# GpSimd adds beta to x after 48 of its 180 trailing scatters, not after all of them: a graph network's node stage on Trainium2

## Chip, cores and metric

The kernel runs on 1 core of one Trainium2 chip, in one launch. The metric is device time in microseconds (us), median over runs. Engines by their names in the profile: PE is TensorE (PEld its weight load), DVE VectorE, ACT ScalarE, POOL GpSimd, SP SyncE, which here only issues DMAs.

## What is computed

A heterogeneous graph attention layer (4 node types, 6 relations, 8 heads), a residual with layer norm, then three graph convolutions with batch norm over the same edges, and a last residual with layer norm. There are N = 6250 nodes of 128 features and E = 106250 edges, sorted by destination. Cut to what matters here:

```python
x = layernorm(x + L0(x, src, dst, node_type, edge_type, ...))
x = layernorm(x + L1(x, edge_index, edge_weight, ...))

# the end of L0, for each node
h = typed_linear(h, Wa, ntype)
gate = sigmoid(skip)[ntype]
y = x + h * gate + x * (1 - gate)
L0 = (y - mu) / sqrt(var + 1e-5) * ln_gamma + ln_beta

# L1, three times
agg = segment_sum((x @ W)[src] * norm, dst) + b
x = relu(batch_norm(agg))        # the last one without relu
```

The outer residual adds x to the normalised y * gamma + beta. The kernel therefore forms x + beta once, for all nodes, and adds it to y * gamma.

## The kernel before

Nodes lie in 49 row tiles of 128, edges in 832 tiles of 128 in the order of their destinations, batched by 16 tiles into NB = 52 batches. The program has these stages, in order of time: tables of keys and values per node (to 650 us or so); the attention over the 52 batches (to 1990); the **node stage**, which this change touches; three graph convolution layers (2286 to 4470); and the last norm.

In the layers the first T1 = 320 edge tiles are done densely. Their weights were written beforehand into a table in HBM, `a_tab`, a piece of the adjacency matrix with 13 chunks of up to 512 columns by 49 row tiles. The table is zeroed early, and then 320 **scatters** on GpSimd (line 481, one indirect DMA for each edge tile, 128 single words, each with `cells_saved`) put the sums in their cells. The first 140 of them are spread over the attention, one before each group of four gathers from batch SB = 17 on (line 494). The other 180 are issued in one loop behind the last gather (lines 505 and 506). Behind that loop GpSimd waits for `y_set` (509) and adds beta to x in the tile `xr`, 128 x 6272 elements in one instruction (510), which raises `xb_ready`. Its next work is the gathers of layer 0 (523), behind `tab_complete`.

VectorE in the node stage: it scales the attention's sums (1391), writes y = x * keep from `xr` and raises `y_set` (1394), adds the four types' parts of h (1406) and takes the moments of each row tile (1411), makes mean, variance and shift of the first normalisation (1419 to 1431), then waits for `xb_ready` (1437). For each chunk of four row tiles it then multiplies by gamma (1442), adds `xr` (1443) and takes the moments (1445); each chunk also waits for ScalarE's first normalise, `y_normed` (683). ScalarE's second normalise writes x1 over `xr`. TensorE turns x1 (954, 957), computes its product with W (981), VectorE scales these rows by the degree into `xr` (1463) and clears the sums (1465). With that, layer 0's dense products (997) can start, as far as their A blocks are loaded. TensorE adds the blocks' own part with the identity (1002) and interleaves the products of gathered edges (969).

SyncE issues in a written order. It waits for `cells_saved` of all 320 scatters and for `types_done` (418, 419). Then, for each layer, it issues NBUF = 4 A blocks of 7 row tiles (416), 12 + 1 stores of h rows to `h_tab` (427, 431) each behind its `hrow_ready`, waits for all of these stores, raises `tab_complete` (433), and issues the remaining 87 A blocks, each behind `a_used`, since there are four buffers.

SyncE's code in front of the layers:

```python
sp.wait_ge(cells_saved, 16 * T1)
sp.wait_ge(types_done, NT)
for l in range(3):
    for b in range(NBUF):
        a_block(l, b)
```

Of the kernel before, what the change touches and what calls it, by code (L numbers as in the profile page):

```python
# [18 lines left out]
NG = TPB // GRP  # L19

T1 = 320
# [3 lines left out]
PACE = 5  # L25
QSTEP = 9
SB = 17
ZB = 2


# [28 lines left out]
def gnn(nc, x, src, dst, etype, ew, ntype, Wk, Wq, Wv, Wa, rel_pri, rel_att, rel_msg, skip, gamma, beta,  # L59
# [13 lines left out]
    NB = ET // TPB  # L73
# [30 lines left out]
    with ExitStack() as ctx:  # L104
# [3 lines left out]
        def sem(name):  # L108
# [16 lines left out]
        sizes = (("big", 2 * TPB * 2 * D), ("relb", TPB * P), ("negs", 4 * P), ("qwin", TPB * D), ("ohT", 2 * GRP * P),  # L125
                 ("bd", 2 * R * D), ("wkqv", 3 * T * D), ("xmT", 4 * T * D), ("qkv", 6 * D), ("square", 5 * P), ("wa", T * D))
        arena = sb("arena", [P, sum(n for _, n in sizes)])
        at, part = 0, {}
        for name, n in sizes:
# [94 lines left out]
        zero_set, a_zeroed, a_rest_zeroed, cells_saved = (  # L224
            sem(n) for n in ("zero_set", "a_zeroed", "a_rest_zeroed", "cells_saved"))
        at = sum(n for _, n in sizes[0:5])
        zero = arena[:, at:at + KB * 256]
        ZT = 61
# [218 lines left out]
        def _(pool):  # L447
# [32 lines left out]
            def scatter(t):  # L480
                G.indirect_dma_start(a_tab, bass.IndirectOffsetOnAxis(cell[:, t:t + 1], 0), tot[:, t:t + 1], None)\  # L481
                 .then_inc(cells_saved, 16)

            def gather(b):
                pool.wait_ge(idx_ready, b + 1)
                pool.sem_inc(gathers_begun, 1)
                if b == SB:
                    pool.wait_ge(a_zeroed, 16 * ZT)
                    pool.wait_ge(a_rest_zeroed, 16 * (NBLK - ZT))
                    pool.wait_ge(tot_ready, 1)  # L490
                    pool.wait_ge(cell_ready, 1)
                for g in range(NG):
                    if b >= SB:
                        scatter(NG * (b - SB) + g)
                    if b >= 3:
                        pool.wait_ge(vw_ready, NG * (b - 3) + g + 1)
                        pool.sem_inc(gathers_begun, 1)
                    for s in range(GRP):
                        t = g * GRP + s
                        G.indirect_dma_start(kv[b % 3][:, t, :], None, kv_tab,  # L500
                                             bass.IndirectOffsetOnAxis(idxr[:, b % 3, t:t + 1], 0))\
                         .then_inc(kv_land[b % 3][g], 16)
            for b in range(NB):
                gather(b)
            for t in range(NG * (NB - SB), T1):
                scatter(t)


            pool.wait_ge(y_set, 1)
            G.tensor_tensor(xr[:, :, :], xr[:, :, :], lnw[:, 1:2, :].to_broadcast([P, NT, D]), ALU.add).then_inc(xb_ready, 1)  # L510

            for l in range(3):
                pool.wait_ge(tab_complete, l + 1)
# [3 lines left out]
                for q in range(GQ):  # L517
# [3 lines left out]
                    for s in range(GRP):  # L521
                        t = T1 + q * GRP + s
# [5 lines left out]
        def _(act):  # L528
# [105 lines left out]
            def attend(b, i, par, peeled):  # L634
                al.at((TPB + NG) * (b - 1) + NG + 2)
                for z in range(ZT + ZB * (b - 1), min(NBLK, ZT + ZB * b)):
                    act.dma_start(a_flat[z, :, :].rearrange("p (a f) -> p a f", a=2),
# [947 lines left out]
```

## Time and profile before

| | |
|---|---|
| median of 3 runs | 4505.61 us (4501.09 to 4509.4) |
| profiled execution, its own time | 4512.08 us |
| its span, first to last instruction | 4510.3 us |
| PE busy | 3479.3 us, 77% of the span |
| POOL busy | 2626.3 us, 58% |
| DVE busy | 2379.0 us, 53% |
| ACT busy | 900.6 us, 20% |
| mean granted TensorE clock | 0.863 |

All times below count from the start of the span, in us. A timeline row has start, duration, engine, line, operation, output<-inputs and count; in brackets stands how long the engine had been idle before it, and what ended that. A row with a count above 1 merges instructions that follow one another. In a row of a DMA the duration is that of the issue on its engine, not of the transfer. Line numbers are those of the kernel before; in the changed kernel the lines from the new constant on are higher by 1, and those behind the new loop by 3.

### The profile page before, as it was taken

The numbers are of one execution on the slowest core, as the hardware profiler recorded it, in microseconds if no ns is written. First come the engines' busy times: TensorE is split into PE (matmuls) and PEld (weight loads), VectorE is DVE, ScalarE is ACT, GpSimd is POOL, SyncE is SP. The second block draws the span as 40 slices with busy tenths as digits, with TensorE's granted clock in tenths as the row PEclk, the third lists the DMA queues.
The fourth block names the chain that finished last, engine by engine and source line by source line (L and its number), as shares of the span: only waits on it lengthen the run. The fifth ranks groups of instructions, "written<-read, shape, count | busy, mean of one in ns | idle before, by whom it ended". The sixth has DMA issues, their size and how long they took to land.

```text
span 4510.3 us, 56344 instructions
## 1 busy us (share of the span) xinstructions
PE 3479.3 (77%) x16302; PEld 2387.8 (53%) x16302; DVE 2379.0 (53%) x7762; ACT 900.6 (20%) x2048; POOL 2626.3 (58%) x2767
## 2 busy tenths in 40 slices
PE   2688856666666666663099999969999978999993
PEld 2577755666665565651055555545555545555552
DVE  2333336667777777774245544455544444554446
ACT  0111124555555555531100000000000000000001
POOL 0000036556777777777447677746777764767772
PEclk8799977777877777777599999979999989999996
DMA  7777757776555555420168788858788867878881
GB/s 261 271 312 305 298 187 272 269 272 198 159 143 157 146 151 152 144 71 1 65 240 299 288 297 302 300 173 308 293 294 296 302 232 256 295 289 297 296 295 49
DMA packets 367669, 1041.17 MB, mean 231 GB/s; under 512 B 77923, under 2 KB 250264, under 8 KB 324610
## 3 DMA queue, kind: packets, MB, share of 16 engines
q1 hardware_dynamic: 251090, 660.52, 40.7%
q0 software_dynamic: 108112, 321.99, 21.2%
q10 hardware_dynamic: 8160, 55.05, 3.2%
q8 instruction: 133, 2.18, 0.2%
q14 instruction: 174, 1.43, 0.1%
HBM read 808.64 MB, written 228.66 MB: 230 GB/s over the span
## 4 chain that ended last, share of the span: by engine, by line
PE 45%; DVE 3%; POOL 1%; issue 1%; DMA 0%; ACT 0%; POOLq 0%; DVEq 0%
PE bank L997 36%; PE bank L969 7%; POOL stage L523 1%; PE bank L1002 1%; DVE nodes L1535 1%; DVE sums L1534 1%; DVE xr L1463 0%; DVE sums L1465 0%; DVE xr L1556 0%; PE bank L981 0%; DMA stage<-h_tab,earr 0%; DVE nodes L1553 0%; DVE sums L1550 0%; PE bank L1015 0%; DVE sums L1503 0%
## 5 line engine op out<-in xcount | busy, mean ns | idle before, releaser
L523 POOL DMA_INDIRECT stage<-h_tab,earr x1536 | 1452.7, 946 | 778.3 <-issue 361.9
L997 PE MATMUL bank<-arena,xr 128*128 128x512 f32 (+1 forms) x3822 | 1693.9, 590 | 9.1 <-DVE xr L1463 9.1
L997 PEld LDWEIGHTS bank<-arena,xr 128*128 128x128 f32 x3822 | 697.8, 191 | 722.2 <-issue 712.6
L1503 DVE TENSOR_TENSOR sums<-sums,bank 128x128 f32 x1536 | 435.6, 284 | 781.1 <-PE bank L969 776.3
L500 POOL DMA_INDIRECT arena<-kv_tab,idxr x560 | 539.9, 964 | 301.7 <-issue 167.8
L1474 DVE TENSOR_SCALAR oh<-iota_j,earr 128x128 f32<-128x128 f32 x1536 | 586.7, 385 | 90.6 <-DVE sums L1494 43.1
L969 PEld LDWEIGHTS bank<-oh,stage 128*128 128x128 f32 x3072 | 408.9, 196 | 236.1 <-issue 190.3
L969 PE MATMUL bank<-oh,stage 128*128 128x128 f32 x3072 | 421.5, 282 | 51.8 <-DMA stage<-h_tab,earr 41.8
L665 ACT ACTIVATE rs<-mv,epsc 128x49 f32<-128x49 f32 (+1 forms) x6 | 1.9, 317 | 2241.2 <-DVE mv L1537 2015.4
L838 PE MATMUL bank<-arena 128*128 128x128 f32 x1664 | 255.9, 310 | 190.1 <-issue 99.1
L481 POOL DMA_INDIRECT a_tab<-tot,cell x320 | 320.9, 1003 | 100.2 <-issue 100.2
L1294 DVE TENSOR_TENSOR sums<-sums,bank 128x256 f32 x832 | 347.8, 418 | 55.0 <-DVE sums L1294 10.4
L838 PEld LDWEIGHTS bank<-arena 128*128 128x128 f32 x1664 | 232.6, 220 | 197.0 <-issue 189.1
L477 POOL DMA_DIRECT2D a_tab<-sums x61 | 32.5, 536 | 518.9 <-ACT stage L561 462.3
L500 POOL DMA_INDIRECT xr<-kv_tab,idxr x272 | 264.5, 972 | 113.2 <-issue 79.6
L852 PE MATMUL bank<-oh,stage 128*128 128x128 f32 x1664 | 292.6, 332 | 34.0 <-issue 21.5
L852 PEld LDWEIGHTS bank<-oh,stage 128*128 128x128 f32 x1664 | 262.7, 240 | 52.5 <-issue 51.0
L1494 DVE TENSOR_TENSOR sums<-sums,stage 128x1 f32 x960 | 154.8, 161 | 219.8 <-DVE sums L1494 62.9
L604 ACT ACTIVATE oh<-iota_j,earr 128x128 f32<-128x128 f32 x832 | 262.5, 386 | 5.4 <-PE bank L855 5.4
L855 PE MATMUL bank<-oh,arena 128*128 128x128 f32 x1664 | 259.5, 308 | 0.0
L855 PEld LDWEIGHTS bank<-oh,arena 128*128 128x128 f32 x1664 | 245.4, 226 | 0.0
L595 ACT ACTIVATE arena<-arena,iota_p 128x512 f32<-128x512 bf16 x208 | 148.1, 712 | 203.6 <-PE bank L838 197.1
(216 smaller groups left out, 3228.4 us busy)
## 6 DMA issues: line engine op xcount, KB each, us to landing
arena<-a_tab SPq DMA_DIRECT2D x273, 1792.0 KB
a_tab<-sums POOLq DMA_DIRECT2D x61, 1792.0 KB, 9.3
a_tab<-arena ACTq DMA_DIRECT2D x30, 1792.0 KB
arena<-q_tab SPq DMA_DIRECT2D x832, 64.0 KB
kv_tab<-stage SPq DMA_DIRECT2D x48, 768.0 KB, 4.7
arena<-rel_d SPq DMA_DIRECT2D x52, 512.0 KB, 5.0
stage<-h_tab,earr POOLq DMA_INDIRECT x1536
h_tab<-xr SPq DMA_DIRECT2D x36, 256.0 KB
```

What stands on the lines that cost most here:

```text
L481: G.indirect_dma_start(a_tab, bass.IndirectOffsetOnAxis(cell[:, t:t + 1], 0), tot[:, t:t + 1], None)\
L500: G.indirect_dma_start(kv[b % 3][:, t, :], None, kv_tab, bass.IndirectOffsetOnAxis(idxr[:, b % 3, t:t + 1], 0))\
L523: G.indirect_dma_start(gring[:, (q % NG) * GRP + s, :], None, h_tab[l], bass.IndirectOffsetOnAxis(src_i[:, t:t + 1], 0)).then_inc(row_land ...
L604: al.inc(S.activation(oh[:, g, s, :], iota_j[:, :], ACT.Abs, scale=-1.0, bias=rel_c[:, bass.ds(c * TPB + (g * GRP + s), 1)]))
L838: last = M.matmul(bank[g % 2][:, s * D:(s + 1) * D], ohT[:, g % 2, s * P:(s + 1) * P], qwin[:, g * GRP + s, :], start=True, stop=True)
L852: M.matmul(o_[s][:, P:2 * P], exw[:, g * GRP + s, :], oh[:, g, s, :], start=True, stop=True)
L855: last = M.matmul(o_[s][:, 0:P], vw[:, g * GRP + s, :], oh[:, g, s, :], start=True, stop=True)
L969: last = M.matmul(bank[q % NG][:, s * P:(s + 1) * P], gring[:, (q % NG) * GRP + s, :], oh[:, q % NG, s, :], start=True, stop=True)
L997: mm = M.matmul(o_[:, 0:cw], xr[:, n, :], abuf[B % NBUF][:, n % KB, 0:cw], start=n == 0, stop=n == NT - 1)
L1294: V.tensor_tensor(w_, w_, d_.rearrange("p (k j) -> p k j", k=2), ALU.add).then_inc(acc_added, 1)
L1474: V.tensor_scalar(oh[:, q % NG, s, :], iota_j[:, :], rel_c[:, t:t + 1], ew_c[:, t:t + 1], ALU.is_equal, ALU.mult).then_inc(wt_ready, 1)
L1503: V.tensor_tensor(w_, w_, bank[q % NG][:, s * P:(s + 1) * P], ALU.add).then_inc(win_added, 1)
```

## The change

GpSimd's loop over the 180 trailing scatters is cut in two. It issues SY = 48 of them, waits for `y_set`, adds beta to x, and then issues the other 132. Nothing else is changed.

```diff
 SB = 17
+SY = 48
 ZB = 2
...
             for b in range(NB):
                 gather(b)
-            for t in range(NG * (NB - SB), T1):
+            for t in range(NG * (NB - SB), NG * (NB - SB) + SY):
                 scatter(t)
 
 
             pool.wait_ge(y_set, 1)
             G.tensor_tensor(xr[:, :, :], xr[:, :, :], lnw[:, 1:2, :].to_broadcast([P, NT, D]), ALU.add).then_inc(xb_ready, 1)
+            for t in range(NG * (NB - SB) + SY, T1):
+                scatter(t)
 
             for l in range(3):
                 pool.wait_ge(tab_complete, l + 1)
```

GpSimd's instructions from the last scatter and gathers of the attention on, before (`a_tab` takes the scatters, `lnw` holds gamma and beta, `arena` here the gathered keys and values):

```order
L481 DMA a_tab<-tot,cell 41746432x1
L500 DMA arena<-kv_tab,idxr 128x256 x4
L481 DMA a_tab<-tot,cell 41746432x1 x180
L510 TENSOR_TENSOR xr<-xr,lnw 128x6272
L523 DMA stage<-h_tab,earr 128x128 x1536
```

And in the changed kernel:

```order
L482 DMA a_tab<-tot,cell 41746432x1
L501 DMA arena<-kv_tab,idxr 128x256 x4
L482 DMA a_tab<-tot,cell 41746432x1 x48
L511 TENSOR_TENSOR xr<-xr,lnw 128x6272
L482 DMA a_tab<-tot,cell 41746432x1 x132
L526 DMA stage<-h_tab,earr 128x128 x1536
```

The add has moved ahead of 132 scatters; the gathers of the layers stay behind both.

SyncE's instructions around the start of the layers, in the changed kernel (`in_x` is x, loaded again into `xr` once the attention has left it):

```order
L408 DMA xr<-in_x 128x32x128
L417 DMA arena<-a_tab 128x3584 x4
L428 DMA h_tab<-xr 128x4x128 x12
L432 DMA h_tab<-xr 106x128
L417 DMA arena<-a_tab 128x3584 x91
```

Nothing has moved there: four A blocks, which wait for the last scatter, stand ahead of the stores of h, and the fifth block (of the 91, 87 belong to layer 0) stands behind them, as before.

## Rows read from the trace of the kernel before

**Rows 1.** The page, section 4: the chain that ended last, by engine and by line

```profile
PE 45%; DVE 3%; POOL 1%; issue 1%; DMA 0%; ACT 0%; POOLq 0%; DVEq 0%
PE bank L997 36%; PE bank L969 7%; POOL stage L523 1%; PE bank L1002 1%; DVE nodes L1535 1%; DVE sums L1534 1%; DVE xr L1463 0%; DVE sums L1465 0%; DVE xr L1556 0%; PE bank L981 0%; DMA stage<-h_tab,earr 0%; DVE nodes L1553 0%; DVE sums L1550 0%; PE bank L1015 0%; DVE sums L1503 0%
```

**Rows 2.** Timeline of VectorE in the node stage

```profile
2011.89 6.69 DVE L1394 TENSOR_TENSOR arena<-xr,keep 128x6272 f32<-128x6272 f32 x1
2018.61 2.16 DVE L1406 SCALAR_TENSOR_TENSOR arena<-bank,gmask,arena 128x128 f32<-128x128 f32 x8
...
2082.75 0.21 DVE L1431 SCALAR_TENSOR_TENSOR shf<-mv,rs 128x49 f32<-128x49 f32 x1
2208.72 0.69 DVE L1442 TENSOR_TENSOR arena<-arena,lnw 128x512 f32<-128x512 f32 x1 [125.76 <-POOL xr L510]
2209.44 0.69 DVE L1443 TENSOR_TENSOR arena<-arena,xr 128x512 f32<-128x512 f32 x1
```

**Rows 3.** Timeline of GpSimd in the node stage

```profile
1956.84 1.00 POOL L481 DMA_INDIRECT a_tab<-tot,cell  x1 [0.30 <-issue]
1958.14 1.21 POOL L481 DMA_INDIRECT a_tab<-tot,cell  x1 [0.30 <-issue]
...
2012.63 6.79 POOL L481 DMA_INDIRECT a_tab<-tot,cell  x1 [0.31 <-issue]
2019.72 0.97 POOL L481 DMA_INDIRECT a_tab<-tot,cell  x1 [0.30 <-issue]
...
2194.30 0.96 POOL L481 DMA_INDIRECT a_tab<-tot,cell  x1 [0.30 <-issue]
2195.28 13.40 POOL L510 TENSOR_TENSOR xr<-xr,lnw 128x6272 f32<-128x6272 f32 x1
```

**Rows 4.** Timeline of ScalarE: its first normalise

```profile
2083.00 18.94 ACT L683 ACTIVATE arena<-arena,shf,rs 128x128 f32<-128x128 f32 x49 [0.78 <-DVE shf L1431]
```

**Rows 5.** SyncE's waits, 1950 to 2500: total, times, longest

```profile
SPq L416 <- DMA a_tab<-tot,cell: 119.5, 1, 119.5
...
SPq L433 <- DMA h_tab<-xr: 2.8, 1, 2.8
```

**Rows 6.** Timeline of SyncE's DMA issues, 1950 to 2500

```profile
2196.46 1.85 SPq L416 DMA_DIRECT2D arena<-a_tab  x4
2273.86 12.30 SPq L427 DMA_DIRECT2D h_tab<-xr  x12
2286.48 0.30 SPq L431 DMA_DIRECT2D h_tab<-xr  x1
```

**Rows 7.** Timeline of TensorE at the start of layer 0

```profile
2286.51 1.86 PE L997 MATMUL bank<-arena,xr 128*128 128x448 f32 x2 [3.39 <-DVE xr L1463]
...
2288.59 31.41 PE L997 MATMUL bank<-arena,xr 128*128 128x448 f32 x78
```

**Rows 8.** Timeline of VectorE in the attention's last batches

```profile
1957.80 1.29 DVE L1271 TENSOR_TENSOR arena<-xr,stage 128x512 f32<-128x512 f32 x2 [0.17 <-ACT stage L623]
```

**Rows 9.** Source line 500, the gathers: ns min/median/max, first and last start

```profile
L500 POOL DMA_INDIRECT xr<-kv_tab,idxr x272: 942/946/1474, 660.6 to 1930.2; - x136
```

**Rows 10.** Busy time by stage (windows), columns in the first row

```profile
core 0: us, PE busy (x) PEld busy (x) DVE busy (x) ACT busy (x) POOL busy (x), PEclk, DMA share, GB/s
...
2209.00:2258.00 49.00, 0.21 (x1) 0.21 (x2) 28.34 (x84) 19.54 (x51) 0.00 (x0) 0.50 0.12 53
2197.00:2215.00 18.00, 0.00 (x0) 0.00 (x0) 6.08 (x16) 0.00 (x0) 11.68 (x1) 0.50 0.98 407
2275.00:2286.00 11.00, 8.12 (x73) 7.92 (x71) 10.45 (x21) 0.00 (x0) 0.00 (x0) 0.98 0.86 242
2286.00:2290.00 4.00, 3.49 (x6) 1.94 (x7) 2.99 (x12) 0.00 (x0) 0.12 (x1) 0.50 0.43 120
2320.00:3003.00 683.00, 645.59 (x2314) 355.21 (x2313) 342.51 (x1380) 1.61 (x4) 469.13 (x496) 0.97 0.76 281
```

**Rows 11.** Source line 477, stores of 1792 KB: us to landing

```profile
DMA to landing us min/median/max: 6.9/9.3/41.1
```

## The prediction

> **What bounds the kernel now.** I read the page's chain first: the matmuls of the three layers and of their edge groups (L997, L969) carry 43% of the span, GpSimd 1%, and no line of the node stage has as much as 1% [rows 1]. So an edit in the node stage pays only if it makes layer 0 start earlier; after that the layers should run as before.
>
> In the timelines of the node stage the reader is to see two engines side by side. VectorE writes y = x times its gate at 2011.89 to 2018.58, which raises y_set, then works through y_rows, and has mean, variance and shift of the first normalisation by 2082.96 [rows 2]. It then stands until 2208.72, 125.8 us, for GpSimd. GpSimd meanwhile issues 180 scatters, one per 1.27 us, from 1956.84 to 2195.26, and only then makes the add, 13.40 us [rows 3]. ScalarE's first normalise ran 2083.00 to 2101.94 and is no cause of the wait [rows 4]. But there is a second reader of the scatters: SyncE waited 119.5 us until all of them had landed, then issued the first four A blocks at 2196.46 [rows 5, 6]. Today these blocks lie ready long before TensorE takes the first at 2286.51 [rows 7]. That cover is what the change uses up.
>
> **The change, part by part.**
>
> The add is neither cheaper nor dearer: 1 instruction, 13.40 us. When is it reached? The scatter at 2012.63 is the 44th of the 180, the one at 2019.72 the 45th [rows 3] ((2012.63 - 1956.84) / 1.27 = 43.9 behind the first); the 48th then starts at 2019.72 + 3 x 1.27 = 2023.5 and ends at 2024.5. y_set was up at 2018.6, so the new place of the wait costs 0, with 5.9 us to spare. The add runs 2024.5 to 2037.9 and VectorE needs it at 2083 or later: the 125.8 us wait is gone. VectorE's next limit is ScalarE: the first four rows of 49 are normalised 4 x 0.39 = 1.6 us after 2083.0, so VectorE restarts at 2084.6 instead of 2208.7, and all that hangs on it (second moments, second normalise, transposes, layer 0's rows of h) comes 124.1 us earlier. The last row of h, written just before 2286.5, is ready at 2162.
>
> Behind the add on GpSimd stand 132 scatters. All of them come 13.4 us later, so the last ends at 2208.7 and not at 2195.3. The scatters are DMA issues; the A blocks (SyncE L416) wait for all 320, and the 13 h_tab stores stand behind these blocks in SyncE's own order. So here is what is late next: SyncE cannot send h_tab, though its rows are ready from 2162, before the last scatter has landed.
>
> To the 13.4 us comes a term that the trace of before shows only in small. VectorE's L1442 and L1443, two SBUF operands each, now run at 2084.6 to about 2113 beside scatters and no longer beside an empty GpSimd. The scatter that began 0.74 us into the 6.69 us L1394 (also two SBUF operands) took 6.79 us instead of 0.97 and ended 0.84 us after it [rows 2, 3]. The one at 1958.14, beside the short L1271, took 1.21 us [rows 3, 8]; the worst gather took 1.474 us against a median of 0.946, 0.53 us more [rows 9]. So a scatter is held until the VectorE instruction ends. VectorE's loop is busy for 28.3 us [rows 10], 23 scatters long; L1442 and L1443 take 1.38 us in some 2.2 us of each chunk, or 0.63 of the time. I take half of that worst case: 23 x 0.63 x 0.27 = **4 us**. Bounds: 0, and 26 instructions x 0.53 = 14 us. For the 6.7 us of L1394 nothing changes, since it meets the 44th scatter in both kernels.
>
> The Trainium skill, "SBUF — State Buffer", section "Who interferes with whom", says that a VectorE instruction with two SBUF inputs contends with a GpSimd instruction that reads SBUF, but that tensor_tensor leaves the generation of DMA descriptors alone, which it marks as inferred. By its second half this term would be 0 and the time 4447.6; the 6.79 us row speaks for the first half, and I go by the row.
>
> So the A blocks go out at 2196.46 + 13.42 + 4 = **2213.9** (call it T).
>
> From T on, with durations from rows:
> - The four blocks are 7.34 MB. In before the DMA engines were 0.98 busy at 407 GB/s for them from 2197 to 2215.3 [rows 10]: the reads end at T + 18.9. The first block should land at about T + 6.9, the shortest landing of any transfer of that size [rows 11].
> - TensorE starts then. Its first 28 row tiles (four blocks of seven) took from 2286.51 to 2288.59 + 54 x 0.40 = 2310.3 in before [rows 7], 23.8 us. So it runs out of blocks at T + 30.7.
> - The 13 h_tab stores, 3.2 MB, queue behind the reads. They moved at 242 GB/s with 0.86 of the engines' time [rows 10], so 3.2 / 0.281 = 11.4 us when nothing paces them, plus 2.8 us for the last to land [rows 5]: T + 33.1, and 0.4 us for the signal and the issue.
> - Only then do the blocks from the fifth on go out (SyncE's order: blocks, h_tab, blocks), and GpSimd's row gathers too. The fifth lands 6.9 us later, T + 40.4. TensorE stands for about 10 us, which in before it did not.
> - After a pause of 3.4 us at 2286 the granted clock was 0.50 for about 4 us [rows 7, 10], the lower of the two levels, 1.2 GHz. I count one such start more, 4 us at half speed: 2 us.
>
> TensorE's 29th row tile is reached at 2213.9 + 40.4 + 2.0 = 2256.3 against 2310.3: **54.0 us earlier**. From there both kernels do the same work. GpSimd's gathers start some 7 us before the fifth block and TensorE needs the first group only at row 40, some 18 us after that start, so it has no lack. The granted clock in the layer was 0.97 [rows 10]; I leave it.
>
> The sum against the profiled execution, 4512.08: 4458.1. That execution lies 6.5 above the median, 4505.61, and by the median the forecast is **4451.6**, 4452 rounded.
>
> So of 125.8 us of waiting less than half is paid out: 124 us earlier on VectorE, of which 70 go back to scatters 17.4 us later, the landing of the blocks, and h_tab behind them.
>
> **The rivals.**
>
> 1. No starving at the fifth block (0.12). If stores and reads share the DMA engines without slowing each other, h_tab is complete before TensorE has used four blocks, and only T + 6.9 + 23.8 counts: 2244.6, 65.7 us earlier, 4440. For it: SyncE issues the 13 stores within some 6 us of T. Against it: the engines were 0.98 busy with the reads alone.
>
> 2. The add is slowed by VectorE (0.11). In before it ran while VectorE did nothing; now it runs beside y_rows. If it took twice its time, every scatter behind it and so T comes 13.4 us later: 40.6 us earlier, 4465. Against: scatters beside y_rows kept their pace of 1.27 us, and L1406 has one operand in PSUM.
>
> 3. Slower than before (0.03). One mechanism: L1442 and L1443 hold the scatters as L1394 did, by 6.79 - 0.97 = 5.8 us in each of 13 chunks, together 76 us in place of my 4. Then T is 2285.9 and the gain of 54 turns into 18 us lost, 4524. It decides from 58 us in all, 4.5 us a chunk. Against: the hold ends with the instruction, and these last 0.69 us, not 6.69.
>
> 4. The whole wait is won (0.02): 4505.6 - 124.1 = 4381.5. It would need SyncE's blocks not to depend on the last scatter; the 119.5 us wait says they do.
>
> 5. The add does not leave the path, within 0.2% (0.02): y_set might be read late or the 48th scatter come before it. Then GpSimd stands for some us, VectorE still goes at 2084.6; only if the scatters end after 2268 is nothing won.
>
> **How the numbers follow.** My own case has 0.70. Its bounds: the hold 0 to 14 us, -4 and +10; h_tab 5 us faster or slower; the slow clock 0 to 4. Together about 4440 to 4467. With rivals 1 and 2 and the noise of the median I give **4434 to 4470**, which leaves out rivals 3 to 5 and the tails. The three runs shown spread by 0.2%; that is about what a measurement tells from no change. Faster by more than that: 0.70 + 0.12 + 0.11 + 0.02 = 0.95; same 0.03 (rival 5 and part of 3); slower 0.02.
>
> **What would show it.** Right: the add at about 2024.5, still 13.4 us long; L1442 starting near 2085 with no GpSimd wait; the last scatter ending near 2213 and SyncE's first blocks right behind; TensorE's first wait in layer 0 for those blocks, a second of about 10 us before the fifth, and from there the same pace. Scatters between 2085 and 2113 longer than 0.97 us. Wrong: scatters slowed by more than 14 us, an add over 14 us, a layer 0 that from row 28 on takes over 5 us more or less than before, or first matmuls that start at 2162 already.

## The result, and the profile after

| | before | changed |
|---|---|---|
| median (runs) | 4507.50 us (4) | 4449.89 us (4), 4448.37 to 4452.93 |
| ratio, 95% interval | | 0.9874 [0.9857, 0.9892] |
| span of the profiled execution | 4510.3 us | 4448.6 us |

The change saves 57.6 us by the medians and 61.7 us between the two profiled executions, of which the one before took 4.6 us more than its median and the changed one 0.4; forecast were 54.0. The page's chain now runs back through the scatters and gathers (L482 has 7% of it), which it did not before [rows 1]:

```profile
PE 52%; POOL 21%; issue 10%; DMA 9%; DVE 5%; SPq 2%; ACT 1%; POOLq 0%; DVEq 0%; ACTq 0%
```

In all rows of the changed kernel the lines are higher by 1 to 3 (L482 is the scatter, L511 the add, L1397 the write of y, L1445 and L1446 the two instructions of VectorE's chunk loop, L1000 the dense product). GpSimd's timeline, against [rows 3]:

```profile
1955.26 0.98 POOL L482 DMA_INDIRECT a_tab<-tot,cell  x1 [0.30 <-issue]
...
2011.46 7.09 POOL L482 DMA_INDIRECT a_tab<-tot,cell  x1 [0.30 <-issue]
...
2022.36 13.48 POOL L511 TENSOR_TENSOR xr<-xr,lnw 128x6272 f32<-128x6272 f32 x1
...
2088.10 0.96 POOL L482 DMA_INDIRECT a_tab<-tot,cell  x1 [0.30 <-issue]
2089.37 1.38 POOL L482 DMA_INDIRECT a_tab<-tot,cell  x1 [0.30 <-issue]
2091.05 1.20 POOL L482 DMA_INDIRECT a_tab<-tot,cell  x1 [0.30 <-issue]
...
2207.76 0.96 POOL L482 DMA_INDIRECT a_tab<-tot,cell  x1 [0.30 <-issue]
```

The add stands in the middle of the scatters, no slower than alone, and with no wait ahead of it. After two of 1.02 and 1.19 us at 2085.29 and 2086.61 the scatters repeat the pattern of the three rows at 2088.10 until 2110: 0.96, 1.38, 1.20 us. VectorE's timeline, against [rows 2]:

```profile
2011.03 6.68 DVE L1397 TENSOR_TENSOR arena<-xr,keep 128x6272 f32<-128x6272 f32 x1
...
2082.00 0.21 DVE L1434 SCALAR_TENSOR_TENSOR shf<-mv,rs 128x49 f32<-128x49 f32 x1
2084.00 0.75 DVE L1445 TENSOR_TENSOR arena<-arena,lnw 128x512 f32<-128x512 f32 x1 [1.78 <-ACT arena L686]
```

The wait of 125.76 us for GpSimd has become one of 1.78 us for ScalarE. SyncE's issues, against [rows 6], and then TensorE, against [rows 7]:

```profile
2209.92 1.85 SPq L417 DMA_DIRECT2D arena<-a_tab  x4
2211.82 24.66 SPq L428 DMA_DIRECT2D h_tab<-xr  x12
2236.53 0.80 SPq L432 DMA_DIRECT2D h_tab<-xr  x1
2240.78 57.12 SPq L417 DMA_DIRECT2D arena<-a_tab  x11
```

```profile
2216.78 1.83 PE L1000 MATMUL bank<-arena,xr 128*128 128x448 f32 x2 [57.70 <-DMA arena<-a_tab]
...
2218.84 21.17 PE L1000 MATMUL bank<-arena,xr 128*128 128x448 f32 x54
2247.92 10.79 PE L1000 MATMUL bank<-arena,xr 128*128 128x448 f32 x24 [7.92 <-DMA arena<-a_tab]
2258.55 1.05 PE L972 MATMUL bank<-oh,stage 128*128 128x128 f32 x8
```

TensorE waits for the first A block, 57.7 us, runs through four blocks (2 + 54 instructions are 28 row tiles), stands 7.9 us for the fifth, and goes on. After both pauses TensorE began at the lower of the two clock levels (windows; PEclk, the granted clock, is the third column from the end):

```profile
2216.00:2220.00 4.00, 3.22 (x6) 1.93 (x7) 0.00 (x0) 0.00 (x0) 0.00 (x0) 0.50 1.02 437
2247.00:2252.00 5.00, 4.08 (x7) 2.08 (x8) 0.00 (x0) 0.00 (x0) 3.77 (x4) 0.60 1.03 413
```

The stores of h went out between the first four blocks and the fifth, at a higher rate than in before (the last column is GB/s):

```profile
2230.00:2236.00 6.00, 6.00 (x17) 3.04 (x16) 0.00 (x0) 0.00 (x0) 0.00 (x0) 1.00 1.14 341
```

The first group of gathered edges, which in before began at 2319.84, begins at 2258.55, 61.3 us earlier; the first products of the other two layers come 61.7 and 61.1 us earlier, and the span is 61.7 us shorter.

### The profile page after: what moved, and what is told of

Its sections match the earlier page's. It is cut to its first block, busy times and chain, and to the rows that moved or that the text cites. A ratio compares the mean times of both kernels' runs of the same rounds, so it can differ in the third digit from the quotient of the medians.

```text
span 4448.6 us, 56344 instructions
## 1 busy us (share of the span) xinstructions
PE 3491.4 (78%) x16302; PEld 2399.4 (54%) x16302; DVE 2378.4 (53%) x7762; ACT 900.5 (20%) x2048; POOL 2624.3 (59%) x2767
## 4 chain that ended last, share of the span: by engine, by line
PE 52%; POOL 21%; issue 10%; DMA 9%; DVE 5%; SPq 2%; ACT 1%; POOLq 0%; DVEq 0%; ACTq 0%
PE bank L1000 36%; POOL arena L501 8%; PE bank L972 8%; POOL a_tab L482 7%; DMA q_tab<-arena 6%; POOL xr L501 4%; DMA negb_d<-arena 2%; PE bank L855 2%; PE bank L858 1%; PE bank L841 1%; POOL stage L526 1%; PE bank L784 1%; PE bank L1005 1%; DVE nodes L1538 1%; PE bank L795 1%
## 5 line engine op out<-in xcount | busy, mean ns | idle before, releaser
L1000 PE MATMUL bank<-arena,xr 128*128 128x512 f32 (+1 forms) x3822 | 1696.0, 590 | 71.4 <-DMA arena<-a_tab 65.6
L1000 PEld LDWEIGHTS bank<-arena,xr 128*128 128x128 f32 x3822 | 698.7, 191 | 785.8 <-issue 771.0
L482 POOL DMA_INDIRECT a_tab<-tot,cell x320 | 320.9, 1003 | 100.1 <-issue 100.1
```

Of the source, the lines that this page charges most:

```text
L1000: mm = M.matmul(o_[:, 0:cw], xr[:, n, :], abuf[B % NBUF][:, n % KB, 0:cw], start=n == 0, stop=n == NT - 1)
```

## The experiments

Two theories stood against each other. **A**: the end follows the last of two things, the last scatter (with the A blocks behind it) or VectorE's rows of h; in the changed kernel it is the last scatter, so nothing that VectorE does matters. **B**: the end follows VectorE's restart. Beside them, **C**: the stop at the fifth block, which A puts down to the stores' place in SyncE's order, comes from DMA engines that are busy with reads.

The first four ran together, with 15 runs of the kernel before at 4510.47 us. VectorE's timelines show where the loop restarts, SyncE's where the first A blocks go out (T), TensorE's the rest. Since the first of the 180 scatters starts up to 8 us apart from one execution to the next (1948.96 in e4, 1956.84 in before), T is also given from the first of the 180 scatters (in e1, which has none there, from the last gather's start + 1.25 us). "Stop" is TensorE's wait for the fifth block, and the last column ends at its first group of gathered edges.

| | SY | median us | restart | T | T from first | first product | stop | T to first group |
|---|---|---|---|---|---|---|---|---|
| changed | 48 | 4449.89 | 2084.0 | 2209.92 | 254.7 | T + 6.9 | 7.9 | 48.6 |
| e1 | 0 | 4508.55 | 2084.3 | 2266.96 | 311.3 | T + 6.9 | 8.4 | 50.5 |
| e2 | 100 | 4449.54 | 2096.8 | 2205.50 | 254.8 | T + 7.0 | 8.8 | 50.8 |
| e3 | 48 | 4437.69 | 2079.1 | 2205.03 | 254.6 | T + 7.3 | none | 39.1 |
| e4 | no add | 4443.75 | 2077.4 | 2193.13 | 244.2 | T + 7.0 | 7.0 | 49.8 |

**e1: the add ahead of all 180.**

```diff
-SY = 48
+SY = 0
```

> The add ahead of all 180 scatters. GpSimd is through with the gathers at about 1955 and must wait for y_set until 2017.7, then add until 2031.2, then issue 180 scatters at 1.262 us with 3.6 us of hold and one gap of 2.7: the last ends near 2265, SyncE's first A blocks go out near 2266. Theory A (the end follows the last scatter, whatever VectorE does): everything from the first A block on 56 to 57 us later than in the changed kernel, about 4506 us, no better than before the change, although VectorE still restarts at 2084. Theory B (the end follows VectorE's restart, which the change moved from 2208.7 to 2084): the same restart, so about 4450.

4508.55 us, ratio to before 0.9996 [0.9987, 1.0005]. VectorE restarts as early as in the changed kernel, and all of the gain is gone. This alone settles A against B. GpSimd's and SyncE's rows:

```profile
2018.40 13.47 POOL L511 TENSOR_TENSOR xr<-xr,lnw 128x6272 f32<-128x6272 f32 x1 [63.02 <-DVE arena L1397]
```

```profile
2266.96 1.80 SPq L417 DMA_DIRECT2D arena<-a_tab  x4
```

GpSimd stands 63 us with 180 scatters behind it. Counted from the end of the gathers T is 56.6 us later; 56 to 57 were worked out.

**e2: the add behind 100.**

```diff
-SY = 48
+SY = 100
```

> The add behind 100 of the 180 scatters. It starts near 2088 and ends near 2101.5, so VectorE restarts 18 us later than in the changed kernel (2083.8). The number of instructions ahead of the last scatter is the same, so it ends where it did, 2208.7 within 2 us. Theory A (last scatter): time unchanged, 4450 within 4. Theory B (VectorE's restart): 18 us later, 4468.

4449.54 us: no change. The wait for GpSimd is back in VectorE's timeline, 19.12 us where the changed kernel waited 1.78, so VectorE restarts 17 us later than it could, at no cost:

```profile
2096.82 0.69 DVE L1445 TENSOR_TENSOR arena<-arena,lnw 128x512 f32<-128x512 f32 x1 [19.12 <-POOL xr L511]
```

T from the first scatter is 254.8 us, against 254.7. Between 48 and 100 scatters ahead of the add nothing is gained or lost.

**e3: the stores ahead of the A blocks, in layer 0.**

```diff
-            sp.wait_ge(cells_saved, 16 * T1)
             sp.wait_ge(types_done, NT)
             for l in range(3):
-                for b in range(NBUF):
-                    a_block(l, b)
+                if l:
+                    for b in range(NBUF):
+                        a_block(l, b)
...
                 sp.sem_inc(tab_complete, 1)
-                for b in range(NBUF, NBLK):
+                if l == 0:
+                    sp.wait_ge(cells_saved, 16 * T1)
+                for b in range(NBUF if l else 0, NBLK):
                     a_block(l, b)
```

> In layer 0 alone, SyncE issues the 13 stores of h and raises tab_complete before it waits for the last scatter, and only then issues A blocks. Theory A (the 7.9 us stop before the fifth A block comes from the stores that queue behind four blocks and hold the fifth back): the stores land near 2165, the stop and the slow clock after it go, TensorE's 29th row tile comes 8 to 9 us earlier, about 4441 us. Theory C (the fifth block is late because the DMA engines are busy with reads, stores or not): a stop of 5 us or more stays, 4447 to 4450.

4437.69 us, 12 us less than e2 and than the changed kernel, the fastest version of the study and faster than both kernels (ratio to before 0.9844 [0.9831, 0.9857]). The stop is gone, so A holds and C falls:

```profile
2144.96 12.25 SPq L428 DMA_DIRECT2D h_tab<-xr  x12
2157.54 0.29 SPq L432 DMA_DIRECT2D h_tab<-xr  x1
2205.03 122.59 SPq L417 DMA_DIRECT2D arena<-a_tab  x21
```

```profile
2212.30 1.83 PE L1002 MATMUL bank<-arena,xr 128*128 128x448 f32 x2 [58.12 <-DMA arena<-a_tab]
...
2214.35 29.98 PE L1002 MATMUL bank<-arena,xr 128*128 128x448 f32 x78
2244.17 1.05 PE L974 MATMUL bank<-oh,stage 128*128 128x128 f32 x8
```

The 78 instructions behind the first tile run in one piece of 29.98 us, where the changed kernel took 21.17 + 10.79 = 31.96 beside its stop: 7.9 of stop and 2.0 of slow clock. From T to the first group it is 9.5 us shorter than in the changed kernel's trace. Against e1 and e2 it is 11.4 and 11.7 us shorter, close to the 12 of the medians, because there the stop and the low clock behind it lasted longer: in the changed kernel the low clock was over after 3 us, in e1 it held through the whole of this window:

```profile
2305.00:2311.00 6.00, 5.58 (x8) 2.71 (x9) 0.00 (x0) 0.00 (x0) 4.48 (x6) 0.50 1.01 405
```

The same 24 products behind the stop took 10.8 us in the changed kernel and 12.2, 12.0 and 11.7 in e1, e2 and e4.

**e4: beta added on VectorE, chunk by chunk, and no add on GpSimd.**

```diff
-            pool.wait_ge(y_set, 1)
-            G.tensor_tensor(xr[:, :, :], xr[:, :, :], lnw[:, 1:2, :].to_broadcast([P, NT, D]), ALU.add).then_inc(xb_ready, 1)
...
-            dve.wait_ge(xb_ready, 1)
...
                 dl.link(V.tensor_tensor(y_, y_, xr[:, n0:n1, :], ALU.add))
+                dl.link(V.tensor_tensor(y_, y_, lnw[:, 1:2, :].to_broadcast([P, n1 - n0, D]), ALU.add))
```

> GpSimd makes no add; VectorE adds beta in its chunk loop instead, 13 further additions of 0.69 us (the sum is rounded in another order). VectorE ends its part some 9 us later, which its slack of 48 us before the last scatter covers. GpSimd's 132 scatters come 13.5 us earlier, less what the 13 new instructions with two SBUF operands hold them, 2 us. Theory A: first A blocks near 2198, 11 to 12 us less than the changed kernel, about 4438. Theory B (VectorE's chain): 9 us later, 4459.

4443.75 us, but its four runs lie between 4433.6 and 4448.4, so the median says only that it is not slower. The trace is sharper: T comes 10.5 us sooner after the first scatter, expected were 11 to 12. Of the 3 us that are missing of the 13.5, about 2 went to the hold, which three instructions with two SBUF operands in each chunk make nearly continuous. As much again went to a slower pace of all scatters in this execution, 1.274 us from one to the next where the changed kernel had 1.262, and 0.7 came back, because the scatter beside the long write of y was held less (6.36 us in place of 7.09). Before, too, ran at 1.273; why an execution has one pace or the other is not shown. GpSimd beside VectorE's loop in e4:

```profile
2083.66 1.19 POOL L482 DMA_INDIRECT a_tab<-tot,cell  x1 [0.30 <-issue]
2085.16 1.15 POOL L482 DMA_INDIRECT a_tab<-tot,cell  x1 [0.31 <-issue]
```

These two alternate until 2113.16; every scatter there takes 1.14 us or more, one 1.41.

**e5 to e12: other chips.** The next two sets of four ran on two other chips, where the kernel before takes 5442.9 and 5447.0 us. They were meant to extend the first set; e9 to e12 are the kernels of e6, e5, e7 and e8 again. The times that their expectations name were worked out for a kernel before at about 4508 us. None of these four kernels ran on the first chip, so what they were to test there stays untested, above all theory A's turning point in e7: that with SY = 140 VectorE's rows become the later of the two sides and the time 4450 to 4458.

> SyncE's order of the third experiment put on the kernel before, where the add is still behind all 180 scatters. There the rows of h are ready only at 2286.5, 90 us after the last scatter. The four A blocks that used to lie ready are now issued at about 2290, behind the wait for the stores, and land 6.9 us later: TensorE's first product of layer 0 comes 10 us later. Theory A (an order of the queue is worth what it is only together with which of the two, scatters or rows, is late): slower than before by 8 to 11 us, 4516 to 4520. If the stores-first order were better by itself: 4500 or less.

> The add on VectorE (fourth experiment) and the stores first (third) together. By theory A the two are terms of one path, the last scatter and what stands between it and the 29th row tile, and add up: 11 to 13 us from the first and 8 to 12 from the second, 4427 within 5 us, the fastest so far. VectorE's rows of h are ready near 2165, still 28 us before the last scatter.

> The add behind 140 of the 180 scatters: it ends near 2151, VectorE's rows of h are ready 78 us later, near 2229, now later than the first A block (2216.8 in the changed kernel). Theory A with the point where it ends (the later of last scatter and VectorE's rows decides): the first product 12 us later, but the stores are no longer packed behind the blocks, so the stop before the fifth block shrinks; 4450 to 4458. Theory B: 4450 + 67 = 4517, since VectorE restarts 67 us later.

> In VectorE's chunk loop the two instructions with two SBUF operands, y times gamma and y plus (x + beta), are replaced by two tensor_scalar instructions with one SBUF operand and constants (y * 1.5, then + 0.5), so gamma and x + beta are left out of the result. If two SBUF operands are what holds a scatter, the scatters beside this loop take 0.96 us like the others, and the 3.6 us of hold go: 4446. The Trainium skill, SBUF - State Buffer, Who interferes with whom, has it the other way round for the generation of DMA descriptors: fp32 tensor_scalar may hold it, tensor_tensor not; then some scatters here stay or become longer, in shorter instructions.

> The kernel of the sixth experiment once more, since there the kernel before itself took 5442.9 us and waits that the profile ascribes to nothing on the core filled the attention. Where the kernel before takes about 4508: theory A says 4425 to 4430, the two gains of the third and fourth experiment (12 us each against the changed kernel) added. Where it takes about 5440 again, this run says nothing on theory A.

> The kernel of the fifth experiment once more, for the same reason. Theory A: 8 to 11 us slower than before, 4516 to 4520, if before is at about 4508.

> The kernel of the seventh experiment once more. Theory A: 4450 to 4458 (the first product waits for VectorE's rows, 12 us later than in the changed kernel, but no stop before the fifth block). Theory B: 4517.

> The kernel of the eighth experiment once more (gamma and x + beta left out of the result, constants in their place). If the hold comes from two SBUF operands: all scatters between 2084 and 2113 at 0.96 us and 3 to 4 us less than the changed kernel, 4446.

The edits: e5 and e10 have the diff of e3 on the kernel before; e6 and e9 those of e3 and e4 together; e7 and e11 have SY = 140; e8 and e12 this one in the changed kernel, which leaves gamma and x + beta out:

```diff
-                dl.link(V.tensor_tensor(y_, y_, lnw[:, 0:1, :].to_broadcast([P, n1 - n0, D]), ALU.mult))
-                dl.link(V.tensor_tensor(y_, y_, xr[:, n0:n1, :], ALU.add))
+                dl.link(V.tensor_scalar(y_, y_, 1.5, None, ALU.mult))
+                dl.link(V.tensor_scalar(y_, y_, 0.5, None, ALU.add))
```

| kernel | first of these chips | against before, us | second | against before, us |
|---|---|---|---|---|
| before | 5442.90 | | 5447.00 | |
| e5, e10: stores first, add behind 180 | 5453.48 | +10.6 | 5458.47 | +11.5 |
| e6, e9: stores first, add on VectorE | 5461.97 | +19.1 | 5469.46 | +22.5 |
| e7, e11: SY = 140 | 5423.74 | -19.2 | 5425.62 | -21.4 |
| e8, e12: SY = 48, two constants | 5408.99 | -33.9 | 5408.78 | -38.2 |

The loss against the first chip lies mostly in the attention: the write of y that raises y_set ended at 2018.6 there and ends at 2896.1 in e5, which has the order of before on GpSimd and VectorE. The two chips show the same picture. Windows of e9 (columns as in [rows 10]), the first in the attention, the second while GpSimd issues its 180 scatters:

```profile
2300.00:2500.00 200.00, 106.28 (x551) 93.63 (x551) 92.51 (x255) 71.15 (x165) 97.68 (x100) 0.63 0.33 96
...
2640.00:2780.00 140.00, 14.18 (x57) 12.41 (x58) 13.20 (x36) 5.57 (x13) 104.68 (x108) 0.51 0.02 1
```

There the last batches of the attention nearly stand still while scatters go out back to back: TensorE is busy for 14 of 140 us. On the chip of the first profiles it was busy for 39 of 63 us beside the same scatters (before, 1956 to 2019). In e12, on the same chip as e9, the add stands behind 48 scatters, and GpSimd issues nothing for 100 us until y_set. The same stretch there, and GpSimd's row:

```profile
2640.00:2780.00 140.00, 86.80 (x415) 60.93 (x415) 99.12 (x277) 32.60 (x68) 37.32 (x26) 0.76 0.08 20
```

```profile
2735.19 13.47 POOL L511 TENSOR_TENSOR xr<-xr,lnw 128x6272 f32<-128x6272 f32 x1 [100.13 <-DVE arena L1397]
```

The same work nearly stands beside scatters and goes on without them; on the other of the two chips it is 16 us of the 140 in e5 and 86 in e8. Already in the attention engines wait longer than on the first chip. The longest sum of waits in e9 from 1500 to 2500 is put down to nothing on the core ("remote"), and GpSimd waits for VectorE behind it:

```profile
DVE negall L1231 <- remote: 457.3, 25, 19.6
POOL arena L503 <- DVE arena L1274: 249.0, 17, 15.8
```

So where nothing interrupts the scatters they end long before VectorE sets y_set, and GpSimd waits for VectorE, not the reverse. In e5:

```profile
2896.15 13.46 POOL L512 TENSOR_TENSOR xr<-xr,lnw 128x6272 f32<-128x6272 f32 x1 [98.91 <-DVE arena L1396]
```

Which of the two sides is late has changed places, and A's rule, the later one decides, can be read with the other sign:

- e5 and e10 met their expectation as a difference, 8 to 11 us slower forecast, 10.6 and 11.5 measured: with the rows of h late, A blocks behind the stores are late too. TensorE waits for them 13.9 us, where in before on the first chip it had waited 3.4 us for VectorE [rows 7] and found them ready:

```profile
3049.87 1.83 PE L999 MATMUL bank<-arena,xr 128*128 128x448 f32 x2 [13.92 <-DMA arena<-a_tab]
```

- e6 missed, 19 us slower where 80 us less than before was forecast, and e9, whose expectation had said that it tells nothing if before takes 5440 again, was 22 us slower. Their two parts are each a loss here: the 11 us of e5, and 13 instructions of 0.69 us, 9 us, on a VectorE that is now the late side; 20 together. The sum of e3 and e4 on the first chip was not measured.
- e7 and e11 missed as well: 50 to 58 us less than before was forecast, 19 and 21 measured. Their gain has nothing to do with the wait of 125.8 us, which does not exist here: a pause in the scatters, while GpSimd waits for y_set, lets the attention's tail go on. The write of y ends at 2896.1 in e5, at 2841.6 in e7 behind 140 scatters, and at 2730.3 in e8 behind 48. Most of that is lost again beside the scatters that are left: VectorE's chunk loop begins at 2961.6, 2941.0 and 2935.7. e8 and e12 gain more than e7 and e11. The changed kernel itself did not run on these chips; e8 has its order on GpSimd and 26 VectorE instructions of 0.41 to 0.43 us in place of 0.69, some 7 us. That the change is a gain there too is thus inferred, not measured.
- e8 and e12 told nothing about the hold: there the last scatter has ended (2917.9 in e12) before VectorE's loop begins (2941.8). Whether instructions with one SBUF operand in that loop would have spared the 3.6 us stays untested.

## Why the prediction was right

Point by point, forecast and measured in the trace of the changed kernel:

| step | forecast | measured |
|---|---|---|
| wait for y_set in its new place | 0 | 0 |
| add starts, its length | 2024.5, 13.40 | 2022.36, 13.48 |
| VectorE restarts | 2084.6 | 2084.0 |
| hold of the scatters by VectorE's loop | 4 us | 3.6 us |
| first A blocks issued, T | 2213.9 | 2209.92 |
| first block landed | T + 6.9 | T + 6.9 |
| stores landed, next blocks issued | T + 33.5 | T + 30.9 |
| fifth block landed | T + 40.4 | T + 38.0 |
| stop before it | about 10 us | 7.9 us |
| slow clock after it | 2.0 us | 2.0 us (3.3, 3.2 and 3.9 in e1, e2 and e4) |
| gain | 54.0 us | 57.6 us (medians) |

The likeliest case came, and the mechanism was right: the scatters' own reader is late next, and e1 shows it at full size. The same restart of VectorE with a later last scatter gives back everything. That VectorE has slack in the changed kernel was argued from 2162 against 2210; e2 spends 17 us of it at no cost. That the time is within 2 us of the forecast, 4449.89 against 4451.6, is in part luck. The profiled executions differ by 7.7 us more than forecast, and most of that is balanced by the 6.5 us by which the profiled execution of before lay above its median, and which the prediction took off, while that of the changed kernel lies only 0.4 us above its median.

The 3.6 us of hold are the sum of what the 17 scatters from 2085.29 to 2108.84 took above 0.96 us. I had built it from half of a worst case, and the mechanism is in the rows: beside a longer instruction with two SBUF operands (L1397, 6.68 us) one scatter takes 7.09 us; in e1, where no scatter runs beside L1397, the longest of all 320 takes 1.424 us. Just ahead of L1397 eleven instructions in one row, with one operand in PSUM (`bank`), run without a break for 6.46 us, and the scatters beside them keep 0.96 us, so it is not a busy VectorE as such (VectorE's row, and one of GpSimd's):

```profile
2004.65 6.46 DVE L1394 TENSOR_TENSOR sums<-sums,bank 128x512 f32<-128x512 f32 x11 [0.16 <-PE bank L941]
2006.41 0.96 POOL L482 DMA_INDIRECT a_tab<-tot,cell  x1 [0.30 <-issue]
```

The Trainium skill, "SBUF — State Buffer", section "Who interferes with whom", has tensor_tensor leave the generation of DMA descriptors alone; here the trace does not agree, and the measured hold stands. Which part of the issue is held, the reading of the indices or the rest, the trace does not tell. The hold is no more than 0.1% of the time.

T came 4.0 us before the forecast, for three small reasons: GpSimd stood 2.1 us further on when L1397 ended (the scatter held by it was the 45th and not the 44th), the 132 scatters ran at 1.262 us and not at 1.273 (1.5 us), and the hold was 0.4 less. The stores were complete 2.6 us before the forecast, counted from T; their rate of 281 GB/s was taken from a stage in which VectorE paced them, and nothing paced them here: 341 GB/s, which makes 9.4 us of the 11.4. Together these are all but 1 us of the gap between 54.0 and the 61.7 of the two traces.

The term for the slow clock came out at 2.0 us, but its reading was short. The prediction looked at 2286 to 2290 only; in before the low level held on (window 2290 to 2292):

```profile
2290.00:2292.00 2.00, 2.00 (x4) 1.01 (x3) 0.00 (x0) 0.00 (x0) 1.70 (x2) 0.50 0.13 33
```

So the low clock at such a start had lasted over 5 us and not 4. In e1, e2 and e4 the term, taken against the 29.98 us of e3 as above, is 3.2 to 3.9 us. That the changed kernel's trace gives just 2.0 is luck.

Of the rivals, the first (no stop at the fifth block) is wrong for this order of SyncE, but e3 reaches it by another: it was worth 65.7 - 54.0 = 11.7 us in the prediction, and 12 us by the medians. What spoke for it in the prediction, 13 store issues within some 6 us of T, did not come either: they took until T + 27.4. The second (the add slowed beside y_rows) fell with 13.48 us. The third needed 58 us of hold. The fourth fell with e1. The fifth was near in kind: y_set was up at 2017.7, the 48th scatter ended at 2022.3, and from 44 scatters ahead of the add downward each one less means 1.26 us of standing. At none, in e1, GpSimd stands 63.0 us and is spared the 6.1 us by which L1397 held one scatter: 56.9, about the 56.6 us measured.

What stays open: why engines wait so long for signals on the two other chips, and why a stream of scatters stops them there; also whether it is the chips or something else in those two launches, for each of them was seen in one launch only. The runs show only that it is so. The prediction holds for the chip of its profile; where the attention's tail ends after the scatters, the place of the add is worth something for another reason.

## What to carry to other kernels

A wait that one engine ends is paid out only up to the next reader of the same queue: list who reads what is pushed back (here SyncE, through the scatters' semaphore), and compute when that reader would have been late. Where loads wait for one thing and stores for another in one issue order, put first what is ready first, and check it in the profile of the kernel as it is: the same reorder gained 12 us behind this change and cost 11 us, on the other chips, in a kernel whose rows were late. Place an instruction that two sides wait for just behind the signal it needs, with a few instructions of margin; a later place, behind 100 of the 180, was free here, while the place ahead of all scatters cost 57 us.

## What the runs showed of the hardware

- A scatter's issue on GpSimd is held by a VectorE tensor_tensor with two SBUF operands until that ends: 7.09 us beside one of 6.68 us, 1.20 to 1.38 us beside those of 0.69 us, 0.96 us otherwise, also beside a tensor_tensor with one operand in PSUM. A reverse effect is not shown: one L1445 took 0.75 us where the others of its size took 0.67 to 0.69.
- How long the low clock lasts at a new start differs between executions of the same order of work: 3 us behind a stop of 7.9 us in the changed kernel, over 5 us behind one of 8.4 us in e1.
- SyncE's twelve store issues took 24.66 us behind four A blocks issued just before, with all rows of h ready, and 12.25 us in e3, where VectorE's rows paced them and no transfer was ahead: issues, too, can wait for the transfers ahead of them.
- The same kernel can differ from chip to chip by more than this change: before took 4507 and 4510 us in the first two launches and 5443 and 5447 us on two other chips, in one launch each, at a mean granted clock of 0.80 against 0.86, with waits that the profile gives to no engine of the core, and with engines that nearly stood while GpSimd issued scatters one behind the other (TensorE busy for 14 of 140 us in e9, for 87 of the same 140 us in e12, on the same chip, where GpSimd paused).
